# A fused two-layer attention and expert network on one core: the stored parts of queries and keys change their layout in memory

## What is computed

```
x = x + tanh(g_xattn[0]) * L0_xattn(ctx, layernorm(x), b, itok)   # keys and values from ctx, a key bias and a length mask
x = x + tanh(g_ffn[0])   * L0_ffn(layernorm(x), ...)              # self attention plus 8 dense experts, top 2 combined
x = x + tanh(g_xattn[1]) * L1_xattn(layernorm(x), ctx, ...)       # keys and values: those of ctx and its own
x = x + tanh(g_ffn[1])   * L1_ffn(layernorm(x), ...)              # causal attention, then 8 routed experts with 1024 hidden features
```

```
scores = einsum('bhqd,bhkd->bhqk', q, k)   # plus bias or mask
attn   = softmax(scores)
out    = einsum('bhqk,bhkd->bhqd', attn, v)
```

## Time and profile before

| | |
|---|---|
| median of 3 runs | 3029.32 us |
| the profiled execution | 3026.3 us |
| its span | 3024.5 us |
| TensorE busy | 2484.4 us (82%) |
| VectorE busy | 1736.7 us (57%) |
| ScalarE busy | 1165.0 us (39%) |
| GpSimd busy | 752.9 us (25%) |
| DMA packets, bytes | 338613, 302.13 MB |
| SyncE's DMA queue (q1) | 42.0% of 16 engines' span |
| mean granted TensorE clock | 0.897 |

### The profile page before, as it was taken

One profiled execution on the slowest core, in us unless ns is written; L12 is line 12 of the kernel. 1 busy time (PEld: TensorE's weight loads), 2 busy tenths in 40 slices (PEclk: granted clock), 3 DMA queues, 4 the chain that ended last, 5 costly groups with the idle time before them and its releaser, 6 DMA issues. The chain is left out here.

```text
span 3024.5 us, 51264 instructions
## 1 busy us (share of the span) xinstructions
PE 2484.4 (82%) x17380; PEld 1619.6 (54%) x17381; DVE 1736.7 (57%) x4456; ACT 1165.0 (39%) x2426; POOL 752.9 (25%) x1410
## 2 busy tenths in 40 slices
PE   2677799899999778899889889999545999999930
PEld 1333455455555444555555567777344767676720
DVE  7566688677777556566666646665446222222238
ACT  1444563233433325565556554555320111111111
POOL 4233331211222131222212222333000222222221
PEclk8777899899899889999899999999855999999975
DMA  8677754443534365665556664666272100100034
GB/s 234 146 159 141 170 102 87 78 73 67 87 63 81 55 117 88 112 109 99 91 97 113 113 109 86 124 127 121 83 271 81 32 31 32 34 31 32 31 124 167
DMA packets 338613, 302.13 MB, mean 100 GB/s; under 512 B 20133, under 2 KB 298447, under 8 KB 338160
## 3 DMA queue, kind: packets, MB, share of 16 engines
q1 hardware_dynamic: 316240, 255.33, 42.0%
q10 hardware_dynamic: 15264, 26.22, 2.5%
q0 software_dynamic: 6912, 17.97, 1.9%
HBM read 205.57 MB, written 93.22 MB: 99 GB/s over the span
## 5 line engine op out<-in xcount | busy, mean ns | idle before, releaser
L1066 DVE TENSOR_REDUCE mx<-s_ps 128x2 f32<-128x512 f32 (+2 forms) x1280 | 796.0, 658 | 408.0 <-PE s_ps L834 189.3
L959 ACT ACTIVATE ex<-t_ps 128x512 f32<-128x512 f32 (+1 forms) x1280 | 684.6, 576 | 427.4 <-PE t_ps L870 393.8
L870 PE MATMUL t_ps<-qs,ks 102*128 102x256 bf16 x2048 | 392.0, 294 | 127.6 <-DMA qs<-mt 109.0
L892 PE MATMUL pv_ps<-ex,va 128*32 128x256 f32 (+1 forms) x5120 | 340.8, 396 | 3.9 <-ACT ex L959 3.5
L870 PEld LDWEIGHTS t_ps<-qs,ks 102*128 102x128 bf16 x2048 | 176.8, 103 | 280.0 <-DMA qs<-mt 118.0
L810 PE MATMUL pre_ps<-wexp,xt 128*128 128x512 f32 x512 | 248.5, 618 | 15.1 <-DVE moe L1134 14.8
L1584 PE MATMUL x_up_ps<-wup,x_rows_t 128*128 x568 | 257.9, 597 | 1.9 <-issue 1.3
L1603 PE MATMUL x_y_ps<-wdn,x_act 128*128 x1136 | 257.0, 379 | 0.9 <-ACT x_act L1630 0.9
L1650 DVE TENSOR_TENSOR x_pre<-x_up_ps,bup 128x512 f32<-128x512 f32 x142 | 98.3, 692 | 233.0 <-PE x_up_ps L1584 233.0
L1000 POOL TENSOR_SCALAR mp<-mx 128x16 bf16<-128x16 f32 x128 | 34.5, 269 | 783.0 <-DVE mx L1066 780.0
L842 PE MATMUL s_ps<-ks,qs 99*128 99x256 bf16 (+1 forms) x1024 | 198.5, 297 | 33.4 <-DVE mx L1066 21.2
(11 more groups left out here) (264 smaller groups left out, 3910.1 us busy)
## 6 DMA issues: line engine op xcount, KB each, us to landing
q_parts<-pq SPq DMA_DIRECT2D x64, 384.0 KB, 6.3
qs<-q_parts SPq DMA_DIRECT2D x64, 384.0 KB, 5.2
qs<-q_parts SPq DMA_DIRECT2D x192, 128.0 KB, 6.0
k_parts<-pk SPq DMA_DIRECT2D x48, 384.0 KB, 2.9
ks<-k_parts SPq DMA_DIRECT2D x48, 384.0 KB
ks<-k_parts SPq DMA_DIRECT2D x144, 128.0 KB
ks<-ctx_k_parts SPq DMA_DIRECT2D x32, 384.0 KB
ks<-ctx_k_parts SPq DMA_DIRECT2D x96, 128.0 KB
```

The costliest lines, as they stand in the source:

```text
L870: last = pe.matmul(dst[:, t * T:(t + 1) * T], key[0:ROWS, h, t * P:(t + 1) * P], qs[q_at][0:ROWS, h, :], start=True, stop=True)
L892: last = pe.matmul(pv_ps[i * VW:(i + 1) * VW, q0:T], val[:, t, k * QH + i, :], e, start=r == 0 and t == 0, stop=r == srcs - 1 and t == NT - 1,
L959: act.activation(ex[:, n % EXPS, 0:w], t_ps[n % 2][:, 0:w], ACT.Exp).then_inc(t_read, 1)
L1066: dve.tensor_reduce(dst, s_ps[n % 2][:, 0:w].rearrange("p (a b) -> p a b", a=parts), AX.X, ALU.max).then_inc(s_read, 1)
```

## The change

The DRAM tensors of the parts are laid out as dimension, part, head, token in place of head, dimension, part, token. The reads of a row of `qs` or `ks` (16 heads x 256 tokens of 2 bytes) then find one run of 8 KB in DRAM, where they found 16 runs of 512 bytes. The stores, which wrote runs of 1536 bytes (3 parts x 256 tokens), write runs of 512 bytes, and by two DMAs, one for each chunk of 8 heads, in place of one; the waits for them count 2 x 16. The planner's costs of the store and read steps are changed with it, so every engine's order is another one.

```diff
@@ -69,8 +69,8 @@
     "XT": [("pe", 0.5), ("act", 0.64)], "KT": [("pe", 0.5), ("act", 1.25)],
     "K": [("pe", 1.8), ("act", 1.25)], "Q": [("pe", 1.8), ("act", 1.25)], "V": [("pe", 1.8), ("act", 0.64)],
     "KSPLIT": [("pool", 3.1)], "QSPLIT": [("pool", 3.1)],
-    "STACKK": [("sp", 0.45), ("wire", 2.6)], "STACKQ": [("sp", 0.45), ("wire", 2.6)],
-    "ROWSK": [("sp", 1.8), ("wire", 8.5)], "ROWSQ": [("sp", 1.8), ("wire", 6.0)], "ROWSC": [("sp", 1.8), ("wire", 8.5)],
+    "STACKK": [("sp", 0.9), ("wire", 4.5)], "STACKQ": [("sp", 0.9), ("wire", 4.5)],
+    "ROWSK": [("sp", 1.8), ("wire", 5.0)], "ROWSQ": [("sp", 1.8), ("wire", 4.0)], "ROWSC": [("sp", 1.8), ("wire", 5.0)],
     "UNBIAS": [("dve", 2.2)], "BPROJ": [("pool", 1.25)],
     "GATE": [("pe", 0.8), ("dve", 0.7)], "GEXP": [("act", 0.25)], "TOP": [("dve", 0.6)],
     "CT": [("pe", 0.3), ("act", 0.4)], "MBIAS": [("pe", 0.9), ("dve", 0.72)], "EXPERT": [("pe", 1.8), ("dve", 1.05)],
@@ -429,9 +429,9 @@
           ln2_g, ln2_b, out):
     dram = lambda name, shape, dt: nc.dram_tensor(name, shape, dt, kind="Internal").ap()
     bias_d = dram("key_bias_parts", [B, 3, T], BF16)
-    q_d = [dram(f"q_parts_{k}", [H, HD, 3, T], BF16) for k in range(NQ)]
-    k_d = [dram(f"k_parts_{k}", [H, HD, 3, T], BF16) for k in range(NKV)]
-    kc_d = [dram(f"ctx_k_parts_{b}", [H, HD, 3, T], BF16) for b in range(B)]
+    q_d = [dram(f"q_parts_{k}", [HD, 3, H, T], BF16) for k in range(NQ)]
+    k_d = [dram(f"k_parts_{k}", [HD, 3, H, T], BF16) for k in range(NKV)]
+    kc_d = [dram(f"ctx_k_parts_{b}", [HD, 3, H, T], BF16) for b in range(B)]
     vc_d = dram("ctx_values", [B, P, NT * H * VW], F32)
     x3_d = dram("x3", [B, P, NT, D], F32)
     h_d = dram("h", [B, P, NT, D], F32)
@@ -651,13 +651,13 @@
                         sp.wait_ge(t_ready, T_AT[("T", v, c, (H - 1, r))] + 1)
 
                 def stack_rows(dst, src, operand, done):
-                    sp.dma_start(dst[0:3 * HD, :, :], src.rearrange("h d a t -> (d a) h t")).then_inc(done, 16)
+                    sp.dma_start(dst[0:3 * HD, :, :], src.rearrange("d a h t -> (d a) h t")).then_inc(done, 16)
                     for r, parts in enumerate(SINGLES):
-                        sp.dma_start(dst[(3 + r) * HD:(4 + r) * HD, :, :], src[:, :, parts[operand], :].rearrange("h d t -> d h t")).then_inc(done, 16)
+                        sp.dma_start(dst[(3 + r) * HD:(4 + r) * HD, :, :], src[:, parts[operand], :, :]).then_inc(done, 16)
 
                 def store_parts(dst, parts, done):
-                    sp.dma_start(dst.rearrange("(c h) d a t -> (h d) c (a t)", c=DC),
-                                 parts[:, :, :, :].rearrange("p c a t -> p c (a t)")).then_inc(done, 16)
+                    for c in range(DC):
+                        sp.dma_start(dst[:, :, c * H // DC:(c + 1) * H // DC, :].rearrange("d a h t -> h d a t"), parts[:, c, :, :]).then_inc(done, 16)
 
                 for step in ORDER["sp"]:
                     name, u, b, k = step
@@ -708,7 +708,7 @@
                         wait_keys_free(u, b, src)
                         if u == 0:
                             sp.dma_start(ks[at][PRODUCTS:BIAS, :, :], bias_d[b].unsqueeze(1).broadcast_to([3, H, T])).then_inc(k_rows[at], 16)
-                        sp.wait_ge(k_stored[part_at], 16 * (nth_part + 1))
+                        sp.wait_ge(k_stored[part_at], 16 * DC * (nth_part + 1))
                         stack_rows(ks[at], k_d[j % NKV] if u else kc_d[b], 1, k_rows[at])
                     elif name == "ROWSC":
                         nth, at = uses_before("kv", (u, b), 0)
@@ -718,7 +718,7 @@
                         if nth_q:
                             v, c = JOBS[j - NQ]
                             sp.wait_ge(t_ready, T_AT[("T", v, c, (H - 1, sources(v) - 1))] + 1)
-                        sp.wait_ge(q_stored[part_at], 16 * (nth_part + 1))
+                        sp.wait_ge(q_stored[part_at], 16 * DC * (nth_part + 1))
                         stack_rows(qs[q_at], q_d[q_at], 0, q_rows[q_at])
                     elif name == "MT":
                         sp.wait_ge(tr_read, TR_AT[step] + 1)
@@ -918,9 +918,9 @@
                         last.then_inc(pre_read[PRE_AT[step] % 2], 1)
 
                     if name in ("K", "KT") and nth_part:
-                        act.wait_ge(k_stored[part_at], 16 * nth_part)
+                        act.wait_ge(k_stored[part_at], 16 * DC * nth_part)
                     if (name == "Q" or name == "XT" and u == 0) and nth_part:
-                        act.wait_ge(q_stored[part_at], 16 * nth_part)
+                        act.wait_ge(q_stored[part_at], 16 * DC * nth_part)
                     if name == "XT" and u:
                         end_pre(act.activation(flat(xt[q_at]), bank[:, :], ACT.Copy))
                     elif name == "OTT":
```

## The result

The changed kernel takes **3040.13 us** (median of 15 runs, 3030.83 to 3049.05); the kernel before, on the same chip, 3028.7 (3019.09 to 3036.19, 15 runs). The ratio is 1.0041, 95% interval 1.0027 to 1.0054: the change costs some 12 us. That is a small loss, told apart from nothing by these runs, and within the half per cent that was called no change. The forecast was 2917 us, and the range ended at 3025.

The account below looks back on a forecast made before the run. It took TensorE as the busiest engine, with about 155 us of its idle time ended by DMAs. -29 - 74 - 56 + 32 + 15 = -112 from 3026.3 gave 2914, with 3 us for the median 2917 us; range 2850 to 3025.

Parts of the forecast that it names:

- the price of a read: Reads of a stack (one DMA of 48 rows, three of 16): from 5.9 to 2.1 us per engine with 8 KB rows.
- it stays 5.9: Upper bound for a stack's read: at 8.4 GB/s an engine, 8 KB rows still take 5.9 us per engine.
- Term 5: SyncE: one more issue for 128 stores and longer waits for stores to land, mostly covered: +15 us, bounds 0 and +70.
- the balance: Per job, on engines carrying `qs<-mt` and stores: packets of parts take 13.8 us before and 11.0 us after.
- The slower rival: Stores clog the engines of `qs<-mt`, deciding at 50 ns per store packet; at 61 ns 3100 us; chance 0.09.
- Term 1: TensorE's wait for the context's keys in unit 2, 30.6 us: -29 us, bounds 0 to -30.6.
- Term 2: TensorE's waits for `qs<-mt` in the attention, 119.2 us: 45 left, -74 us, bounds -119 and +18.
- Term 3: TensorE's clock in the three stretches from 60 to 1700 us, rising as gaps go: -56 us, bounds 0 and -85.
- Term 4: Given back where TensorE next waits for other engines, such as VectorE in unit 0: +32 us, bounds 0 and +60.
- the sign of being wrong: TensorE's waits for `qs<-mt` at 119 us or more would show the prediction wrong.
- last sign of being wrong: Waits for `qs<-mt` gone, but others of equal size, by VectorE or for `q_parts`, in their place.
- The rival of no change: Reads into 96 partitions not bound by packet count, so long rows win nothing: 3034 us, within 15 us of now; chance 0.09.

Follow-up runs that it names:

- high block: Kernel before, with only the block of 48 rows of qs and ks moved to partitions 48 to 95 and the single parts to 0 to 47: 2944.24 us, ratio 0.9729.
- padded store: Kernel before, with 16 dimensions of a head padded to 17 in DRAM and one store for each half, packets still 1536 bytes: 3186.52 us, ratio 1.052.
- single even one: Kernel before, with DRAM as half, part, partition, token: one store of 512-byte packets, outermost dimension 128, rows read as two 4 KB runs: 2955.97 us, ratio 0.9768.

## Why the prediction was wrong

**What each piece was worth.** Under the old order, long reads took 1.9% off (0.9814) and the new stores put 4.2% on (1.0228 / 0.9814); the new order then took 1.8% off (1.0041 / 1.0228). On 3028.7 us that is -56, +125 and -57, +12 together. The prediction had -127 for the reads (terms 1 to 4), +15 for the stores and nothing for the order. The size of a piece hangs on which is taken first: with short reads the stores cost 4.6%.

**The step that failed first: the price of a read.** "at 23 GB/s one takes 0.36 us, a stack 2.1 us." The pages give another value, an estimate that puts all of the difference down to the stacks. Over its span q1 was busy 42.0% of 16 x 3024.5 us before, 20,325 us; with long reads alone it was busy 37.2% of 16 x 2954.8, 17,587 us. The difference over 144 stacks and 16 engines is 1.2 us: a stack takes 4.7 us per engine, where it took 5.9 and 2.1 were predicted. The value came from the earlier trace rows, loads in another place; the bound that "it stays 5.9" was nearer. Two things make a stack slow, and neither alone. The run length: 1.2 us in the kernel, though only 0.1 to 0.5 us alone in the queue. And the partitions that it writes: with the high block and short reads q1 is busy 38.5% of 16 x 2946.9 us, 18,153, which by the same working is 0.9 us less a stack. Against the time the partitions did more (0.973, and 0.977 to 0.957 with long reads).

**The step that failed second: what the stores cost.** Their own size was right: half the engines, 31.6 ns a packet where 35 was taken, 96 x 31.6 = 3.0 us where 3.4 was. The failure is in how it was charged: +15 us, where the runs have +125. Term 5 charged +15 us for SyncE and let the engines' time ride on the balance "2 x 2.1 + 2 x 3.4 = 11.0 us" against 13.8. With the read at 4.7 the balance is 2 x 4.7 + 2 x 3.0 = 15.4 us: it is above 13.8, not below. The slower rival's threshold, 50 ns a store packet, falls with it: (13.8 - 9.4) / 192 = 23 ns, and 31.6 is past it. The rival had the mechanism and a threshold that leaned on the wrong read.

The same sum, an estimate from rows for each kernel under the old order and the old partitions, against what it measured (an old store is 17.2 / 16 = 1.1 us; over 16 engines the short packets are 768 x 26 / 16 = 1.2 us; the padded store is 43.1% x 16 x 3 / 8 = 2.6 us):

| kernel | reads | stores | sum us a job on an engine that carries stores | ratio |
|---|---|---|---|---|
| long reads, old stores | 2 x 4.7 | 2 x 1.1 | 11.6 | 0.981 |
| long reads, short packets on 16 | 2 x 4.7 | 2 x 1.2 | 11.8 | 0.978 |
| before | 2 x 5.9 | 2 x 1.1 | 14.0 | 1 |
| the change's layout | 2 x 4.7 | 2 x 3.0 | 15.4 | 1.023 |
| padded, 1536 bytes on 8 | 2 x 5.9 | 2 x 2.6 | 17.0 | 1.052 |
| new stores, short reads | 2 x 5.9 | 2 x 3.0 | 17.8 | 1.046 |

The sum puts them in order but for a neighbouring pair at either end, and the layout of the change stands above the kernel before, as measured. It is a reading after the fact, not a test.

Point by point. Term 1 (-29): the wait for the context's keys rose by 3.1; long reads alone gave -20.1, the stores took it back. Term 2 (-74): -20.8 with long reads alone, +40.3 with the layout under the old order (131.5 + 28.0 = 159.5 us, past the sign of being wrong), -15.6 in the change, by the order. Term 3 (-56): in the three stretches the clock went from 0.84, 0.93, 0.94 to 0.89, 0.92, 0.93, a gain in the first alone, and TensorE's idle time was 236.1 where 240.6 stood, so little came of it. Term 4 (+32) came without the gain that it was to follow: the idle time of L842, 24.2 + 9.2 = 33.4 us before, is 32.3 + 34.2 = 66.5 in the change. Most of that is the order's doing: the group of 96 rows stands 9.7 us with the layout under the old order and 37.0 with the old layout under the new one. It is what the prediction's last sign of being wrong named, waits of another kind in place of those for DMAs. Term 5 (+15): the stores cost 4.6% with short reads, some 133 us (3157.59 less 3024.7). SyncE's waits for stores did not grow to 300 us. With the layout under the old order they grew from 181.2 to 144.3 + 81.8 = 226.1; the new order brings them down to 66.4, and to 39.0 with the old layout:

```profile
SPq L725 <- ACT mt L954: 505.7, 89, 25.3
...
SPq L721 <- DMA q_parts<-pq: 44.3, 25, 3.4
...
SPq L711 <- DMA k_parts<-pk: 22.1, 13, 9.5
```

The layout loses 2.3% under the old order and the change 0.4%, so the order is worth 1.8% to the new layout where it was worth 0.4% to the old one. The prediction gave it no term.

The rival of no change named the time (3034), but by luck. It had part of the cause of the slow reads, the bytes' way into 96 partitions, and put the flat result down to reads that win nothing; the runs show a gain of 1.9%, a loss of 4.2% and 1.8% from the order, which happen to cancel. The Trainium skill's rule on how many engines a DMA uses ("DMA: Bandwidth & Descriptors", the section on the semaphore's 16) was cited for the stores, and the traces agree with its number: DMA rows at 5 tenths where the outermost dimension is 8, at 9 where it is 128. That these are the engines which `qs<-mt` uses as well rests on the page alone; no row tells which engines a DMA is on.

## What to carry to other kernels

Look at what a DMA's two sides have as outermost dimension before its packets: here stores on half the engines cost 5.2% with the packets untouched, while three times as many packets over all engines cost nothing that shows. Take the price of a transfer from a row that writes the same partitions, since 48 rows low, 48 rows high and the same bytes over 128 partitions took 4.34, 3.42 and 2.92 us; moving a block to other partitions is a free edit that won 2.7% before the change, though only 0.4% after it. But a price taken alone in the queue isn't the price in the kernel: long runs won 1 to 8% there and a fifth of a stack's time here. And where a change trades two large costs on one shared resource, write the balance with each price at both its ends: one wrong end turned the sign here.

## What the runs showed of the hardware that I had not expected

- Reads into 48 partitions, alone in the queue, hardly care for run length (4.34 against 4.43 us, 8 KB against 512 bytes), but for which partitions (3.42 against 4.34).
- A 512-byte packet of a store takes 26 to 32 ns, a 1536-byte one 63: three times the bytes take twice the time or a little more. The 61 ns of a 512-byte packet in the earlier trace rows, where stacks, a store and a load share the queue, are no price of a packet by itself: in the kernel a stack's time fell by a fifth with longer runs and by a sixth with other partitions.
- A DMA's packets under 512 bytes count the engines that it uses: 16 for the old store, 8 for each new one, 3 for `qs<-mt`.
- An issue on SyncE takes longer for the stores with an outermost 8 (0.58 us at the median, where the old one and the single even one take 0.38), and single ones take up to 6.9 us. What holds them no row names.
